# Row maxima of two attention heads by two 64-row matmuls from the high halves of q and k

## What is computed

```python
xn = _layernorm(x)
q = einsum('bqm,muh->bquh', xn, Wq) + bq          # k and v the same way, 8 heads
q = _interleaved_rope(q, cos, sin) * SCALE        # k too
scores = einsum('bquh,bkuh->buqk', q, k)          # k, v repeated for the 4 heads of a group
scores = where(abs(pos_q - pos_k) <= 128, scores, NEG)
probs = softmax(concatenate([scores, sink_logits], -1))
attn = einsum('buqk,bkuh->bquh', probs[..., :-1], v)
s = einsum('bquh,uhm->bqm', attn, Wo) + bo
x = x + s * silu(fp8_round(xn) @ W_ffn.T + b_ffn)
```

## Time and profile before

| | before |
|---|---|
| median of 3 runs | 1925.35 us |
| span of the profiled execution | 1928.5 us |
| PE busy, of the span | 94% |
| weight loads busy | 89% |
| DVE, ACT, POOL busy | 71%, 73%, 61% |
| mean granted TensorE clock | 0.983 of full speed |

### The profile page before, as it was taken

The page is one execution under the profiler, slowest core; times in us unless marked ns, Lnnn a source line. Parts: engine busy times, 40 slices in busy tenths (PEclk is TensorE's granted clock), DMA queues, the critical chain, the costliest instruction groups (busy, mean ns, idle before and its releaser), DMA issues.

```text
span 1928.5 us, 48655 instructions
## 1 busy us (share of the span) xinstructions
PE 1818.4 (94%) x13199; PEld 1707.6 (89%) x13199; DVE 1373.2 (71%) x4883; ACT 1406.3 (73%) x3764; POOL 1183.6 (61%) x1511
## 2 busy tenths in 40 slices
PE   3499999999999999999999999999999999999997
PEld 2399998999989999899989999899998999889996
DVE  8776776777767777767767777577777676776775
ACT  3277777777767777777867777677877787777775
POOL 4465656666566666666656666566666665665654
PEclk9699999999999999999999999899999999999999
DMA  5200000000000000000000000000000000000000
GB/s 191 82 8 2 0 1 25 12 2 0 13 20 5 1 0 18 19 2 0 1 19 18 2 0 1 30 7 2 0 18 19 2 1 1 18 24 2 0 1 17
DMA packets 20889, 28.07 MB, mean 15 GB/s; under 512 B 1344, under 2 KB 19264, under 8 KB 20544
## 3 DMA queue, kind: packets, MB, share of 16 engines
q1 hardware_dynamic: 20672, 25.45, 4.0%
HBM read 21.25 MB, written 4.19 MB: 13 GB/s over the span
## 4 chain that ended last, share of the span: by engine, by line
PE 86%; DVE 5%; issue 4%; ACT 1%; DMA 0%; DVEq 0%; POOLq 0%; POOL 0%; ACTq 0%
PE pv_bank L1042 26%; PE ring L974 15%; PE ring L1016 10%; PE acc L1063 9%; PE score L1028 8%; PE score L1030 7%; PE ring L983 5%; PE ring L1051 3%; PE ring L995 2%; PE ring L964 1%; PE ring L1001 1%; DVE junk L772 1%; DVE neg_max L781 1%; DVE sink_arg L786 1%; DVE proj L760 1%
## 5 line engine op out<-in xcount | busy, mean ns | idle before, releaser
L1042 PEld LDWEIGHTS pv_bank<-v,stage 128*128 128x128 f32 x5136 | 682.5, 192 | 4.7 <-issue 1.1
L1042 PE MATMUL pv_bank<-v,stage 128*128 128x65 f32 x5136 | 674.0, 266 | 0.9 <-DVE o_norm L800 0.9
L772 DVE CUSTOM_DVE_ANT_0 junk<-ring,mask 128x384 bf16<-128x384 f32 (+1 forms) x1036 | 507.0, 490 | 224.9 <-PE ring L1016 198.3
L529 ACT ACTIVATE stage<-score 128x512 f32<-128x512 f32 x640 | 357.0, 588 | 283.1 <-PE score L1030 282.3
L464 POOL TENSOR_SCALAR_AFFINE_SELECT stage<-stage 128x512 f32<-128x512 f32 x384 | 243.2, 641 | 425.1 <-ACT stage L529 425.1
L1016 PE MATMUL ring<-kT_high,qT_full 128*128 128x384 f32 (+1 forms) x1036 | 398.9, 385 | 16.6 <-DVE proj L760 15.4
L444 POOL TENSOR_TENSOR qk_parts<-turned,qk_parts 128x320 fp32r<-128x320 f32 x263 | 227.3, 864 | 207.0 <-ACT qk_parts L564 207.0
L552 ACT ACTIVATE qT_high<-ring,own_rows 8x128 fp32r<-8x128 f32 x1032 | 284.9, 345 | 13.7 <-PE ring L1001 7.3
L1028 PE MATMUL score<-qT_full,kT_high 128*128 128x512 f32 x640 | 267.7, 418 | 16.1 <-issue 14.9
L760 DVE TENSOR_TENSOR proj<-ring,bias 128x384 f32<-128x384 f32 x264 | 145.7, 552 | 183.7 <-PE ring L974 183.2
L1030 PE MATMUL score<-qT_high,kT_low 72*128 72x512 f32 x640 | 256.3, 400 | 0.0
(11 more groups left out here) (110 smaller groups left out, 3282.4 us busy)
## 6 DMA issues: line engine op xcount, KB each, us to landing
x_in<-in_x SPq DMA_DIRECT2D x13, 512.0 KB, 3.6
x_res<-in_x SPq DMA_DIRECT2D x18, 256.0 KB, 3.3
out<-x_res SPq DMA_DIRECT2D x16, 256.0 KB, 2.2
stage<-in_w_qkv SPq DMA_DIRECT2D x4, 768.0 KB, 5.0
gate<-in_x SPq DMA_DIRECT2D x4, 512.0 KB, 4.1
stage<-in_w_o SPq DMA_DIRECT2D x4, 512.0 KB, 3.6
bias<-in_b_qkv SPq DMA_DIRECT2D x1, 1152.0 KB, 6.6
bias<-in_b_qkv SPq DMA_DIRECT2D x1, 384.0 KB, 7.8
```

Of the source, the lines that this page charges most:

```text
L529: nc.scalar.activation(prob[:, q % 2 * 3 + n, :], score[(FIRST[q] + n) % 2][:, :], ACT.Exp) \
L772: nc.vector.tensor_tensor_reduce(junk[:, h % 2, 0:cols], ring[h % 2][:, 0:cols], mask[:, m0:m0 + cols], 1.0, LOWEST, ALU.add, ALU.max, row ...
L1042: last = nc.tensor.matmul(pv[:, h, :], prob[:, q % 2 * 3 + n, h * P:(h + 1) * P], v[:, par, k, :], start=(n == 0), stop=(n == len(BLOCKS[q ...
```

## The change

The two rows of a pair of heads are computed by two matmuls of 64 partitions each. The first head of the pair takes q's high part from `qT_high` (partitions 0 to 63), the second takes it from `qT_full` (partitions 64 to 127), each against the copy of k's high part in the same partitions; q's low part no longer enters the row maximum. `row(0)` now issues rows 0 and 1, `row(2)` rows 2 and 3, and `row(1)` and `row(3)` are gone. The number of matmuls and of increments is the same.

The waits are now those of a pair. `row(0)` waits for `qT_high` instead of `qT_full`, and also until DVE has read the projection. `row(2)` waits until DVE has finished the maxima of both heads 0 and 1. On ACT, `q_high` is issued right behind `q_full` instead of at the end of the iteration. On PE, the pairs are placed anew among the other pieces: row(0) comes behind `weighed(0)` in the common cases and behind `weighed(2)` in the one iteration of a batch in which a new x is transposed.

```diff
             def q_full(b, q):
                 at(act, s_qfull_pe, TILES, b, q + 1)
                 nc.scalar.activation(qT_full[:, q, :], ring[0][:, :], ACT.Copy).then_inc(s_qfull_done, 1)
-
-            def q_high(b, q):
                 at(act, s_qfull_done, TILES, b, q + 1)
                 nc.scalar.activation(qT_high[0:D, q, :], qT_full[D:2 * D, q, :].bitcast(F32), ACT.Copy) \
                     .then_inc(s_qhigh_done, 1)
@@ in the step of ACT @@
-                    if b1:
-                        q_high(*back(it + 1, q, 1))
@@ score_rows @@
                 if h == 0:
-                    at(pe, s_qfull_done, TILES, b, q + 1)
-                elif h == 1:
+                    at(pe, s_qhigh_done, TILES, b, q + 1)
                     at(pe, s_proj_done, TILES, it + 2, now + 1)
                 else:
-                    at(pe, s_max_done, TILES * GROUP, b, GROUP * q + h - 1)
+                    at(pe, s_max_done, TILES * GROUP, b, GROUP * q + h)
...
-                nc.tensor.matmul(ring[h % 2][:, 0:cols], qT_full[:, q, h * P:(h + 1) * P],
-                                 kT_high[:, par, k0 * P:k0 * P + cols], start=True, stop=True).then_inc(s_max_pe, 1)
+                nc.tensor.matmul(ring[0][:, 0:cols], qT_high[0:D, q, h * P:(h + 1) * P],
+                                 kT_high[0:D, par, k0 * P:k0 * P + cols], start=True, stop=True).then_inc(s_max_pe, 1)
+                nc.tensor.matmul(ring[1][:, 0:cols], qT_full[D:2 * D, q, (h + 1) * P:(h + 2) * P],
+                                 kT_high[D:2 * D, par, k0 * P:k0 * P + cols], start=True, stop=True) \
+                    .then_inc(s_max_pe, 1)
@@ the order of the pieces on PE: new x @@
-                        row(0)
                         weighed(0)
                         weighed(1)
                         maxima_turn()
                         projection()
                         weighed(2)
+                        row(0)
                         weighed(3)
-                        row(1)
                         heads_turn()
+                        outwards()
                         row(2)
-                        outwards()
-                        row(3)
@@ q == 0 @@
                         maxima_turn()
+                        weighed(0)
                         row(0)
-                        weighed(0)
                         weighed(1)
-                        row(1)
                         weighed(2)
                         row(2)
                         heads_turn()
                         weighed(3)
-                        row(3)
                         outwards()
```

## The result

| | before | after |
|---|---|---|
| median of four runs (lowest to highest) | 1925.32 us (1919.59 to 1928.68) | 2162.56 us (2156.27 to 2166.47) |
| span of the profiled execution | 1928.5 us | 2160.7 us |
| mean granted TensorE clock | 0.983 | 0.955 |

What follows compares the result with a forecast made beforehand. PE was taken to bound the kernel, busy through a 26.8 us step; waits for the projection's read, two maxima and max_rows add 1.32 us a step, 84 us over 64 steps, plus 6 for late DVE work: 2016 us, range 1930 to 2090.

Steps and rivals of the forecast that it cites:

- T1: Start of the first pair on PE, forecast 0.82, 0.82, 1.14 and 1.11 us after E for q = 3, 0, 1, 2.
- T2: Start of the second pair on PE, forecast 2.60, 2.82, 2.17 and 2.49 us after E for q = 3, 2, 0, 1.
- the end: Where the next piece follows (output projection at q = 3); forecast +0.49, +0.33, +0.39, +0.11 us for q = 3, 2, 0, 1.
- E: Moment on PE at which the projection's last matmul gives way to the next piece; 1164.89 in the profiled q = 3.
- The switch between halves and whole: On PE, changing between 64-partition and full-array matmuls: 0 to 0.05 us each, taken as 0; at 0.05, 26 us more.
- The projection's read at q = 0: First pair waits for DVE's read of the projection, taken to start at E + 0.20 and release PE at E + 0.82.
- The chain of two maxima: Main term: second pair waits for two DVE maxima in a row, 1.71 us after T1 with 384 columns, 1.35 with 256.
- q_high on ACT: Moved ahead of max_rows, its 0.63 us delays heads_turn; next piece at E + 2.60, 0.07 behind the maxima at q = 3.
- late DVE work: Iterations where DVE has other work before the projection's read: 0 to 0.15 us for half of 256, taken as 6 us.
- The second matmul: Second matmul of a pair on PE, taken at 0.12 us; rival: free, 31 us less, 1985 us, chance 0.17.
- The clock: Rival: granted TensorE clock falls behind new waits, up to 96 us on top, 2080 us and above, chance 0.05.
- The gain on the other side: Rival: PE's own work covers the maxima between T1 and T2, 0.91 us less a step, 1867 us, chance 0.15.

Runs made afterwards that it cites:

- full-height pairs: Changed kernel with its order, waits and early q_high, but both matmuls of a pair over all 128 partitions: 2100.39 us, 1.0876.
- full-height pairs with the late `q_high`: Changed kernel with 128-partition matmuls, q_high back at the end of ACT's iteration and row(0) waiting for q_full; also called the waits and the order alone: 2060.71 us, 1.0672.
- short maxima: Changed kernel, each DVE maximum over 128 keys instead of 256 or 384: 2109.58 us, 1.0919; likewise with 128-partition pairs and late q_high: 1999.57 us, 1.0351.
- the earlier `max_rows`: Changed kernel with max_rows ahead of the high halves on ACT, except at q = 1 and in the iteration of a new x: 2158.84 us, 1.1188.
- the move alone: Kernel before, only with q_high right behind q_full on ACT, no PE wait or order changed: 2026.15 us, 1.0494.
- one half at a time: Kernel before, order and waits kept, each row's matmul from one half, 64 partitions high: 2409.41 us, 1.25.

## Why the prediction fell short, by its own steps

T1, T2 and the end are counted from E, in us, in the undisturbed step at the full clock:

| | T1 forecast, measured | T2 | end | end before |
|---|---|---|---|---|
| q = 3 | 0.82, 0.82 | 2.60, 2.81 | 4.16, 4.54 | 3.67 |
| q = 2 | 1.11, 1.30 | 2.82, 3.04 | 4.38, 4.77 | 4.05 |
| q = 0 | 0.82, 1.10 | 2.17, 2.51 | 3.06, 3.47 | 2.67 |
| q = 1 | 1.14, 1.23 | 2.49, 2.64 | 3.18, 3.42 | 3.07 |

The four ends are 2.74 us later than before where 1.32 was forecast: 0.92 of the difference is in T2, 0.50 behind it.

**The switch between halves and whole was the failed step.** It was bounded by 0 and 0.05 from the nearest row, a matmul behind one with 64 columns, and taken as 0. That row changes the columns, not the partitions, and had nothing to say. At q = 2 the first pair waits for nothing (DVE's read of the projection ended at 1300.39):

```profile
1299.84 0.83 PE L1040 MATMUL pv_bank<-v,stage 128*128 128x65 f32 x6
1300.60 0.44 PE L1011 MATMUL ring<-kT_high,qT_high 64*128 64x384 f32 x1
```

Measured: 0.17 longer ahead of this pair (0.76 for 0.59), 0.09 with four short matmuls at q = 1, 0.18 more between `heads_turn` and the pair at q = 3 (0.37 for 0.19), 0.18 to 0.19 behind it (1.36 and 1.37 for the 1.18 of two `weighed`). A pair therefore takes about 0.73 us of PE's time where two separate full-height rows took 0.52 and two adjacent ones 0.46. The weight loads show one place of it (PEld at q = 2; the pair and the next load):

```profile
1300.60 0.18 PEld L1011 LDWEIGHTS ring<-kT_high,qT_high 64*128 64x128 f32 x1
1300.60 0.18 PEld L1013 LDWEIGHTS ring<-kT_high,qT_full 64*128 64x128 f32 x1
1300.97 0.74 PEld L1040 LDWEIGHTS pv_bank<-v,stage 128*128 128x128 f32 x6 [0.19 <-issue]
```

The loads of the pair start with its matmuls and not ahead of them, and the next load 0.37 later, when the pair has streamed. Of the 1.42 us missed a step, the switch makes some 0.9 (0.18, 0.17 and 0.09 ahead of T2 at q = 3, 2 and 1, and the 0.50 behind it); 64 x 0.9 is 58 us. That this is close to the 62 us that the full-height pairs gave back is a coincidence: in clean steps they gave back some 36, in part because such a pair itself takes 0.46 where the halves take 0.37, and the rest came with the clock. The rule of the Trainium skill, TensorEngine Tiling (Array Packing), section Key Properties, that a change of mode drains TensorE, speaks of this; the trace agrees, at 0.17 to 0.19 on each side, three to four times the 0.05 that I had weighed it with.

**The projection's read at q = 0.** T1 was built on DVE's start at E + 0.20, read at q = 3 and used for all. At q = 0 DVE starts at E + 0.49 (1285.78), and it did so before: its row of that iteration in the kernel before, not among the rows of the prediction, has E at 1144.91 and DVE's read 0.49 later:

```profile
1145.40 0.56 DVE L760 TENSOR_TENSOR proj<-ring,bias 128x384 f32<-128x384 f32 x1 [1.06 <-PE ring L974]
```

It was there to be read, and is 0.28 us a step, 18 us. At q = 3 the 0.82 was exact.

**The chain of two maxima** was right in its length: 1.71 and 1.35 forecast, 1.74 (1.99 at q = 3 with ACT's wait in it) and 1.41 measured. That it holds PE is shown for full-height pairs with the late `q_high`, at 61 us. In clean steps of the changed kernel it holds PE at q = 2 and hardly elsewhere. There the times agree in part by luck: with short maxima it is still 1.35 and 1.41 us from T1 to T2 at q = 0 and 1, by PE's own work and its switches.

**q_high on ACT** was priced at 0.07 us at q = 3 only. Inside the changed kernel that is right (2.44 for the 2.41 forecast). But I held it against the maxima's chain and never asked what it costs alone: 97 us. It makes the forecast seem to hang on one chain where there are two of nearly the same length, and that fits with how little the shorter maxima or the earlier `max_rows` bring alone at q = 3; no run has both. At q = 3 of a batch's sixth step the move alone costs 1.30 us and the whole change 1.53, where the prediction had 0 to 0.15 for late DVE work on top of its 0.49. At q = 3 of the eighth step both cost about 2.6 on average, with 2 to 9 us of each such iteration at 1.2 GHz.

**The second matmul** was taken at 0.12 and is free (0.00 to 0.01). The rival was right, and so is the rule of the Trainium skill, TensorE: Matmul & The Clock Gate, section Packing small matmuls. It brought nothing beyond the forecast: the pair as a whole takes 0.37, where 0.26 + 0.12 was forecast, since its first matmul no longer hides in the pieces around it.

**The clock** had 0.05 as a rival and is part of the result, some 35 us. My bound, a gap of 0.60 us that left the clock at 1.00, looked at single gaps. PE in the changed kernel ahead of the second stretch shown at the top:

```profile
884.06 0.44 PE L1011 MATMUL ring<-kT_high,qT_high 64*128 64x384 f32 x1 [0.63 <-DVE proj L756]
...
885.79 0.68 PE L1011 MATMUL ring<-kT_high,qT_high 64*128 64x384 f32 x1 [0.26 <-DVE row_max L768]
...
886.41 2.82 PE L1040 MATMUL pv_bank<-v,stage 128*128 128x65 f32 x12
```

The clock is back at 2.4 GHz from 868.4 after a gap of 2.47 us that ended at 864.02, and falls again at 885.5. In between PE has only the gap of 0.63 us, and that of 0.26 ends as the clock falls; none is of 2 us as in the earlier trace rows. `weighed` then takes twice its time. The loop spent 27.4 us at 1.2 GHz in the kernel before, 39.8 with the move alone, 75.1 with full-height pairs, 155.6 after the change and 372 with one half at a time. So it grows with the time that PE loses in small pieces, though not strictly: with the waits and the order alone it is 32.5, at a larger loss than that of the move. What exactly decides it stays open.

**The gain on the other side** didn't come: T2 was never near the 1.16 and 1.05 us from T1 that it needed. With the short maxima in the changed kernel it was still 1.35 to 1.53 at q = 0, 1 and 2, so a shorter chain alone would not have brought it.

The sum, put right: 1.32 forecast, + 0.9 for the switch, + 0.28 for the read at q = 0, + some 0.24 in small terms and + 0.19 between the output projection and the next E, gives the 2.93 of a clean step. Of the 146 us by which the forecast of 2016 fell short, 103 are this difference of 1.61 us in 64 steps (some 60 the switch, 18 the read at q = 0, 25 the small terms, whose cause I haven't traced) and some 35 the clock; the rest is small.

## What to carry to other kernels

Two matmuls on two halves of the array run at once, but a single pair between full-height matmuls costs more than it saves here, 0.73 us for 0.52: whether it pays where many such pairs stand together, no run here shows. An operation that no row of the trace shows needs a bound that admits it may cost much more than its nearest relative. Before work of two heads is joined under one wait, write down the loop through the other engine, and read each engine's start in every kind of iteration, not in one. Where two chains of the same length hold a point, price each alone and together: 97 and 130 us alone were 170 together.

## What the hardware did that I had not expected

- Two matmuls of 64 partitions on different halves and banks start 0.00 to 0.01 us apart, and so do their weight loads.
- Going to 64 partitions and back costs 0.17 to 0.19 us on each side at the full clock; over a program with 1036 single rows it was 480 us, clock included.
- The granted clock was 0.91 in a stretch of 18 us that the profile calls busy from end to end, and 0.53 in one of 7 us behind waits of PE of 0.63 and 0.26 us. Time lost between overlapping matmuls is not idle time in the profile.
